# Graph layer on one core: the beginning reordered (zeros without DMA, W1 ahead of W2, rows turned ahead of the first sums, rstd ahead of the additions)

## The reference

```python
agg = jax.ops.segment_sum(edge_attr, dst, num_segments=12500)     # 12500 x 48
h = jnp.maximum(layernorm(x), 0.0)
c = jnp.concatenate([h, agg], axis=1)                             # 12500 x 176
a = silu(c @ W1 + b1)                                             # 256 wide
a = silu(a @ W2 + b2)                                             # 256 wide
out = x + h + a @ W3 + b3                                         # 128 wide
```

## Time and profile before

| | us |
|---|---|
| median of 3 runs | 303.75 (303.45 to 303.93) |
| the profiled execution | 302.05 |
| its span, first to last instruction | 300.3 |
| busy: PE, DVE, ACT, POOL | 283.9, 249.2, 222.5, 112.2 |

### The profile page before, as it was taken

How to read it: one execution, slowest core, us unless ns; L and a number is a source line. 1 busy time by engine, 2 the same in 40 slices (tenths; PEclk the granted TensorE clock), 3 DMA queues, 4 the chain that set the end, 5 groups by cost and what they waited for, 6 DMA issues and landing times.

```text
span 300.3 us, 12188 instructions
## 1 busy us (share of the span) xinstructions
PE 283.9 (95%) x4370; PEld 256.4 (85%) x4371; DVE 249.2 (83%) x615; ACT 222.5 (74%) x434; POOL 112.2 (37%) x243
## 2 busy tenths in 40 slices
PE   7596879999999999999999999999999999999995
PEld 3584758899999999999999999999999999999794
DVE  7956988799888898889988898889988889875551
ACT  5555267887788877888777887888777887789662
POOL 4062345243433435334343334434444343542200
PEclk9899599999999999999999999999999999999999
DMA  6998999368655786557855678556875568631112
GB/s 171 293 264 242 170 215 253 85 204 244 192 164 156 228 244 177 161 158 237 243 162 151 182 240 233 157 155 189 244 232 151 150 203 244 199 109 34 33 32 58
DMA packets 79418, 54.49 MB, mean 181 GB/s; under 512 B 2997, under 2 KB 78863, under 8 KB 79253
## 3 DMA queue, kind: packets, MB, share of 16 engines
q1 hardware_dynamic: 79397, 54.25, 64.9%
HBM read 46.29 MB, written 6.40 MB: 175 GB/s over the span
## 4 chain that ended last, share of the span: by engine, by line
PE 78%; issue 8%; ACT 4%; POOL 3%; DMA 2%; DVE 1%; POOLq 1%; SPq 1%; ACTq 0%; DVEq 0%
PE agg_ps L1054 18%; PE z L1122 16%; PE z L1104 7%; PE z L1105 7%; PE z L1108 7%; PE agg_ps L1057 4%; PE z L1084 4%; PE z L1089 3%; PE z L1085 3%; PE z L1086 3%; PE z L1090 3%; POOL agg_carry L462 3%; PE tp L1068 3%; DMA raw<-in_edge_attr_dram 2%; ACT xn L543 1%
## 5 line engine op out<-in xcount | busy, mean ns | idle before, releaser
L462 POOL TENSOR_TENSOR agg_carry<-staged,agg_carry 48x42 f32 x196 | 69.5, 354 | 91.4 <-ACT staged L511 58.3
L1054 PEld LDWEIGHTS agg_ps<-onehot,raw 128*48 128x48 f32 x1560 | 75.2, 128 | 12.6 <-issue 12.5
L1054 PE MATMUL agg_ps<-onehot,raw 128*48 128x42 f32 x1560 | 78.9, 218 | 3.9 <-DVE onehot L729 3.7
L1057 PE MATMUL agg_ps<-onehot,raw 128*48 128x42 f32 x1568 | 79.3, 218 | 0.6 <-DMA raw<-in_edge_attr_dram 0.6
L729 DVE TENSOR_TENSOR onehot<-window,rel 128x1176 f32<-128x1176 f32 (+1 forms) x57 | 76.9, 1350 | 3.0 <-DVE stats L704 2.7
L1057 PEld LDWEIGHTS agg_ps<-onehot,raw 128*48 128x48 f32 x1568 | 75.8, 129 | 0.8 <-issue 0.8
L443 POOL TENSOR_TENSOR rstd<-vareps,minus_half 112x4 f32<-112x4 f32 (+1 forms) x28 | 39.5, 1411 | 77.4 <-DVE vareps L714 77.4
L1122 PE MATMUL z<-w,h 128*112 128x128 f32 (+1 forms) x448 | 55.9, 278 | 0.8 <-ACT h L575 0.8
L1122 PEld LDWEIGHTS z<-w,h 128*112 128x112 f32 (+1 forms) x448 | 50.4, 176 | 2.4 <-ACT z L571 1.1
L575 ACT ACTIVATE h<-z,b2c 128x448 f32<-128x448 f32 (+1 forms) x56 | 35.4, 633 | 20.3 <-PE z L1108 17.7
L543 ACT ACTIVATE xn<-x_t,nmr,rstd 112x128 f32<-112x128 f32 (+1 forms) x112 | 45.6, 478 | 0.9 <-DVE nmr L722 0.8
(11 more groups left out here) (128 smaller groups left out, 421.6 us busy)
## 6 DMA issues: line engine op xcount, KB each, us to landing
raw<-in_edge_attr_dram SPq DMA_DIRECT2D x55, 672.0 KB, 6.0
x_t<-in_x_dram SPq DMA_DIRECT2D x27, 224.0 KB, 6.3
out_dram<-out_t SPq DMA_DIRECT2D x27, 224.0 KB, 6.1
agg_carry<-agg_carry SPq DMA_DIRECT2D x3, 504.0 KB, 12.8
dst_rows<-in_dst_dram SPq DMA_DIRECT2D x1, 512.0 KB
raw<-in_edge_attr_dram SPq DMA_DIRECT2D x1, 288.0 KB, 3.5
dst_rows<-in_dst_dram SPq DMA_DIRECT2D x1, 256.0 KB, 2.8
out_t<-in_L_gnn_W_dram SPq DMA_DIRECT2D x1, 256.0 KB, 7.4
```

Source lines behind the costliest of these rows:

```text
L462: pool.tensor_tensor(into, staged[:, parity, n, :], into, ALU.add).then_inc(s_added, 1)
L1054: mm = pe.matmul(banks[0:ED, bass.ds(offsets[at - first], WINDOW)], edges, into, start=False, stop=True, skip_group_check=True, tile_posit ...
L1057: mm = pe.matmul(stage[ROW2:ROW2 + ED, at * WINDOW:(at + 1) * WINDOW], edges, into, start=(at == 0 and j == 0), stop=True, skip_group_chec ...
```

## The change

All of it lies in the first steps.

- GpSimd zeroes columns 896 to 8064 of `agg_carry` in four memsets of 1792 columns, behind its iota; ScalarE zeroes all behind, 4544 columns, in one instruction. The three DMAs and the second piece of ScalarE are gone.
- On SP's queue W1 goes ahead of W2, and so do the second half of the edges of batch 1 and `x` of tile 1; W1 and W2 get semaphores of their own. ScalarE and DVE split W1 first and W2 later, `layer1(0)` waits for W1 alone, `layer2(0)` for W2, `activate1(0)` and `layer3(0)` for the small constants.
- ScalarE turns the relative targets of all lots ahead of the staged sums of batch 0 and splits W1 ahead of them too.
- PE turns all four lots of rows ahead of the sums of batch 0, with five matmuls without use between (`WARM1`); eight in place of six ahead of the sums of batch 1 (`WARM2`).
- GpSimd reads the places of batches 0 and 1 at once, then makes `rstd(0)`, then adds batch 0 and batch 1, then makes `rstd(1)`.
- DVE takes the statistics of tile 1 ahead of `carry_over(0)`.
- In DVE's step 1 both one-hots of batch 2 and the split of W2 come ahead of `shift_of_norm(1)`.
- `carry_over` waits for the zeros once, at tile 0.

```diff
-    WARM0, WARM1 = 3, 6
+    WARM0, WARM1, WARM2 = 3, 5, 8
...
-        COPIED, COPIES = 6 * TILE, 3
-        ZEROED = 4 * TILE
+        ZEROED = 18 * TILE
+        CARRY0 = 2 + (ZEROED - POOL_ZEROS) // (4 * TILE)
...
-            sp.dma_start(w2_in, W2.rearrange("(m p) n -> p m n", p=P)).then_inc(s_weights, 16)
-            sp.dma_start(w1x_in, W1[0:D, :]).then_inc(s_weights, 16)
+            sp.dma_start(w1x_in, W1[0:D, :]).then_inc(s_w1, 16)
             for a in (0, ROW2):
-                sp.dma_start(w1e_in[a:a + ED, :], W1[D:D + ED, :]).then_inc(s_weights, 16)
+                sp.dma_start(w1e_in[a:a + ED, :], W1[D:D + ED, :]).then_inc(s_w1, 16)
             load_edges(1, 1, 1)
+            load_x(1, 1)
+            sp.dma_start(w2_in, W2.rearrange("(m p) n -> p m n", p=P)).then_inc(s_w2, 16)
...
-            for c in range(COPIES):
-                sp.dma_start(zeros_to[:, c, :], agg_carry[:, ZEROED + COPIES * COPIED:NT * TILE]).then_inc(s_carry0_dma, 16)
...
             pool.iota(tile_i[:, :], pattern=[[1, TILE]], base=0, channel_multiplier=0).then_inc(s_pool_zero, 1)
+            for a in range(POOL_ZEROS, ZEROED, 4 * TILE):
+                pool.memset(agg_carry[:, a:a + 4 * TILE], 0.0).then_inc(s_carry0, 1)
...
             pool.wait_ge(s_off0, 1)
-            nodes = nodes_of(0)
-            pool.wait_ge(s_carry0, 2)
-            add_staged(0, 0, nodes, range(0, EARLY))
+            nodes = [nodes_of(b) for b in range(2)]
             rstd_of(0, 0)
-            add_staged(0, 0, nodes, range(EARLY, HALF))
+            pool.wait_ge(s_carry0, CARRY0)
+            pool.wait_ge(s_carry0_act, 1)
+            add_staged(0, 0, nodes[0])
+            add_staged(1, 1, nodes[1])
             rstd_of(1, 1)
...
-            clear_carry(ZEROED + COPIES * COPIED, NODES)
+            clear_carry(ZEROED, NODES)
             rel_of(0)
             act.wait_ge(s_dst, 64)
             for c in range(1, ROWS):
                 rows_of(c)
-            clear_carry(POOL_ZEROS, ZEROED)
-            rel_of(1)
-            stage_sums(0, 0)
-            for c in range(2, ROWS):
+            for c in range(1, ROWS):
                 rel_of(c)
-            act.wait_ge(s_weights, WEIGHTS)
...
+            stage_sums(0, 0)
...
             normalize(0, 0)
+            act.wait_ge(s_w2, W2_LOADS)
+            act.activation(w2_hi[:, :, :].rearrange("p m n -> p (m n)"), w2_in.rearrange("p m n -> p (m n)"),
+                           ACT.Copy).then_inc(s_w_hi, 1)
             stage_sums(1, 1)
...
             make_onehot(1, 1, 1)
+            weights1_lo()
             dve.wait_ge(s_smallT, 1)
...
-            weights_lo()
+            load_stats(1, 1)
             dve.wait_ge(s_rel, ROWS)
...
-                    load_stats(1, 1)
                     dve.wait_ge(s_stats, 2)
                     aggregate_stats(1, 1)
                     make_onehot(2, 0, 0)
+                    make_onehot(2, 0, 1)
+                    weights2_lo()
                     shift_of_norm(1, 1)
-                    make_onehot(2, 0, 1)
...
+            turn_rows(1)
             pe.wait_ge(s_off0, 1)
+            turn_rows(2)
+            for _ in range(WARM1):
+                pe.matmul(tp[:, 0:P], ident[:, :], ident[:, :], start=True, stop=True)
             offsets = offsets_of(0)
-            turn_rows(1)
+            turn_rows(3)
             sum_tile(0, 0, offsets)
-            for c in range(2, ROWS):
-                turn_rows(c)
...
-            for _ in range(WARM1):
+            for _ in range(WARM2):
                 pe.matmul(tp[:, 0:P], ident[:, :], ident[:, :], start=True, stop=True)
             sum_tile(1, 1, offsets)
```

More of the change, by code:

```diff
@@ L144, in gnn_kernel @@
         POOL_ZEROS = 2 * TILE
-        COPIED, COPIES = 6 * TILE, 3
-        ZEROED = 4 * TILE
-        assert ZEROED + (COPIES + 1) * COPIED == NT * TILE and LOOP[0] * TILE == ZEROED
+        ZEROED = 18 * TILE
+        CARRY0 = 2 + (ZEROED - POOL_ZEROS) // (4 * TILE)
+        assert (ZEROED - POOL_ZEROS) % (4 * TILE) == 0
         gen_onehot = onehot[:, 2:4].rearrange("p s e w -> p (s e w)")[:, 0:PER * TILE].rearrange(
@@ L204, in rows_turned @@
             return banks[c][:, 0:PER * (P if c < FULL_ROWS else LAST_G)].rearrange("p (j r) -> p j r", j=PER)
-        s_weights = sem("weights_loaded")
+        s_w1 = sem("w1_loaded")
+        s_w2 = sem("w2_loaded")
         s_const = sem("const_loaded")
@@ L451, in nodes_of, with add_staged @@
                 return nodes
-            def add_staged(b, parity, nodes, which=range(HALF)):
+            def add_staged(b, parity, nodes):
                 pool.wait_ge(s_staged, b + 1)
                 wait(pool, s_carried, b)
-                if isinstance(b, int) and b == LATE_ZEROS:
-                    pool.wait_ge(s_carry0_dma, 16 * COPIES)
-                for n in which:
+                for n in range(HALF):
                     wait(pool, s_added, added(b, n))
@@ L465, in step @@
                 parity = turn % 2
-                if has(i, 0, NT):
+                if has(i, 0, NT) and not (isinstance(i, int) and i == 1):
                     nodes = nodes_of(i)
@@ L579, in activate1 @@
                 n = PER * nodes_p(t)
+                if isinstance(t, int) and t == 0:
+                    act.wait_ge(s_const, CONSTS)
                 for m in range(M):
@@ L736, in make_onehot, with weights1_lo, weights2_lo @@
                 onehot_of(i, parity, half).then_inc(s_onehot, 1)
-            def weights_lo():
-                dve.wait_ge(s_w_hi, 4)
[L741 to L747, removed]
+            def weights1_lo():
+                dve.wait_ge(s_w_hi, 3)
+                dve.wait_ge(s_pool_zero, 3)
+                for lo, whole, hi in ((w1x_lo[:, :], w1x_in, w1x_hi[:, :]),
+                                      (w1e_lo[0:ED, :], w1e_in[0:ED, :], w1e_hi[0:ED, :])):
+                    dve.tensor_tensor(lo, whole, hi.bitcast(F32), ALU.subtract).then_inc(s_w_lo, 1)
+            def weights2_lo():
+                dve.wait_ge(s_w_hi, 4)
+                dve.tensor_tensor(w2_lo[:, :, :].rearrange("p m n -> p (m n)"), w2_in.rearrange("p m n -> p (m n)"),
+                                  w2_hi[:, :, :].rearrange("p m n -> p (m n)").bitcast(F32),
+                                  ALU.subtract).then_inc(s_w_lo, 1)
             dve.wait_ge(s_rel, 1)
@@ L857, in carry_over @@
                 dve.wait_ge(s_added, added(t + 1))
-                dve.wait_ge(s_carry0_act, 2)
-                if isinstance(t, int) and t == LATE_ZEROS - 1:
-                    dve.wait_ge(s_carry0_dma, 16 * COPIES)
+                if isinstance(t, int) and t == 0:
+                    dve.wait_ge(s_carry0, CARRY0)
+                    dve.wait_ge(s_carry0_act, 1)
                 wait(dve, s_carried, t)
@@ L1076, in layer1 @@
                 if isinstance(t, int) and t == 0:
[L1077 to L1080, removed]
+                    pe.wait_ge(s_w_lo, 2)
+                    pe.wait_ge(s_w_hi, 3)
                 for m in range(M):
@@ L1095, in layer2 @@
                 n = PER * nodes_p(t)
+                if isinstance(t, int) and t == 0:
+                    pe.wait_ge(s_w_lo, 3)
+                    pe.wait_ge(s_w_hi, 4)
                 pe.wait_ge(s_h1, M * t + M)
@@ L1116, in layer3 @@
                 last = isinstance(t, int) and t == NT - 1
+                if isinstance(t, int) and t == 0:
+                    pe.wait_ge(s_const, CONSTS)
                 pe.wait_ge(s_seeded, t + (2 if last else 1))
```

15 lines of the change are left out of this document (4 added, 11 removed).

## The result

| | before | after |
|---|---|---|
| median of 16 runs each, us | 303.4 (301.89 to 305.94) | 306.33 (305.78 to 307.2) |
| the profiled execution | 302.05 | 305.78 |
| its span | 300.3 | 304.1 |

The ratio is 1.0096 (95% interval 1.0077 to 1.0115): the change makes the kernel slower, by 2.9 us against a forecast of 5.2. The time measured, 306.33, lies in the forecast range (301.0 to 310.3), nearer to rival 2 (307.6) than to the forecast itself (308.9).

The account below looks back on a forecast made before the run. PE is busy throughout from 60 to 280 us, so only the start of layer 1 of tile 1 counts: sums of batch 1 +5.4, with the tail +5.2, on the median 303.75 give 308.9 us; range 301.0 to 310.3.

Parts of the forecast that it names:

- rival 2: DVE's first small steps: DVE gets in at each end of a memset, 4.8 us late, so 307.6 us; chance 0.17.
- the entry: Start of layer 1 of tile 1 on PE, 41.81 us before; its shift was forecast at +5.2 and carried unchanged.
- Rival 1: Beginning of the kernel: the memsets do not hold DVE and the change is faster, 301.6 us; chance 0.28.
- Two of its signs: Trace signs: L643 about 6.5 us, prediction wrong as a whole if it ends before 5; `staged_row` at 15.7.
- one lock: DVE's first small steps: four memsets without pause hold DVE until 10.2 us, making the offsets 6.1 us late.
- 2.3 and 0.7 for the clock: PE from offsets to sums of batch 0: turning and warming 2.3 us, plus 0.7 for the lower clock.
- the bound for full clock: Sums of batch 0 on PE: 2.8 us if the clock is full, against the 3.8 us taken in the forecast.
- Small products: PE between the sums of batches 0 and 1: small products 1.64 us, then 16 warming instructions 2.13 us.
- The tail: End of sums of batch 1 to layer 1 of tile 1, 18.2 us: -1.37 - 0.87 + 0.6 + 1.4 = -0.2.
- The wait of `nmr(1)`: DVE in norm 1: `rstd(1)` behind all fourteen additions makes DVE wait 2.3 us against 0.91, a term of +1.4.
- The shift: Change of the start of layer 1 of tile 1, +5.2 us, carried unchanged to the end and put on 303.75.
- The zero copies: Three DMA transfers removed: the room they leave gives nothing, as no wait up to layer 1 of tile 1 ends with a load.

Follow-up runs that it names:

- before_memsets: The kernel before with only the zeroing changed: four GpSimd memsets behind the iota, ScalarE all behind, no zero copies; 306.36 us, ratio 1.0106.
- late_memsets: The changed kernel with its four memsets moved behind GpSimd's reading of the first places; 301.43 us, ratio 0.9962 to the kernel before.
- one_memset: The changed kernel with its four memsets made into one of 7168 columns; 306.93 us, ratio 1.0148 to the kernel before.
- before_late: The kernel before without zero copies, zeros written by ScalarE and thirteen GpSimd memsets of 48x448 behind the register loads of batch 0; 301.75 us, ratio 0.9936.
- dve_order: `late_memsets` with DVE's second one-hot of batch 3 behind `carry_over(1)` and the first of batch 4 behind the split of `hT` of tile 1; 300.27 us, ratio 0.9894.
- best1: Changed order, `dve_order`'s one-hot move, six unused matmuls behind tile 1's transposes, thirteen late memsets of 448 columns, three more tiles zeroed by ScalarE; 297.21 us, 0.9805 to before.
- warm_entry: `late_memsets` with ten matmuls without use on PE behind the transposes of tile 1; 300.23 us, ratio 0.9914 to the kernel before.

## Why the prediction was right, and where not

**The direction and its cause were right.** The memsets hold DVE, the offsets come late, and PE's chain up to the entry moves with them. `before_memsets` alone shows it, and `late_memsets` is its counterpart. The range says little for it, as it was wide enough to hold a gain too. Rival 1's case, with no hold on the path, is the one that `late_memsets` comes near to: a gain of 1.1 us, where the rival had 1.9 to 2.4.

**Two of its signs failed.** L643 was to last about 6.5 us, and the prediction was to be wrong as a whole if it ended before 5. Its successor L639 lasts 1.82 and ends at 3.66, so by the letter of that sign the prediction fails. In the kernel before the step ahead of it (L641) was the one held up to 3.65; here that step got through in 0.17, so DVE was one step further on when the long memsets began. They held others, from `g_pair` at 4.17 on, so the sign was tied to one instruction where it should have been tied to the chain. `staged_row` came at 14.37, not 15.7. The rest came about: sums 0 at 18.38 (18.5), sums 1 at 25.3 (26), no stop of GpSimd put down to "issue", 1.58 us ahead of `nmr(1)` (2), the entry at 45.24 (47), the clock at 0.50 from 11 to 17.

**The step that failed first was how a held DVE gets in.** The forecast took "one lock" over the whole run of memsets, 6.1 us; its own rival 2 had DVE get in at each end, 4.8 us, and 4.98 was measured. `one_memset` shows what 6.1 belongs to: `staged_row` at 15.32, 5.9 late. The row that spoke for it, L641's 2.02 us, was read as held over several instructions, and such a hold shows again in the kernel after (L639, 1.82 us over the ends of four short memsets). What failed was to carry it over to the four long ones: DVE got in at each of their ends. The Trainium skill, "SBUF — State Buffer", Who interferes with whom, has the ports held "for the whole instruction"; with that the trace agrees four times over for the long memsets, and L639 does not fit it. One detail differed from rival 2: not every small step was held. L645, which has two inputs and 0.16 us, ran while the second memset did, and the third hold fell on the two CASTs, so rival 2's 4.8 was met in part by other steps than it named.

**From the offsets to sums 1.** From the offsets (14.57, the end of `staged_row`) to sums 0 (18.38) PE turned, warmed and turned for 3.8 us, where 2.3 and 0.7 for the clock stood: the clock was at 0.50 from 11 to 17. In return it was back at 1.00 from 18, and sums 0 took 2.7 us, near the 2.8 of the bound for full clock, and not 3.8. Small products 1.64 and warming 2.05 came as forecast, with a gap of 0.57 ahead of them that the sum had left out. Together sums 1 began at 25.3, 1.0 sooner than forecast. Part of that closeness is luck: offsets and sums 0 came 2.2 us cheaper than in the sum, the turning and the gap 1.4 dearer.

**The tail** went from 18.2 to 17.2, by -1.0 and not -0.2. Three of four terms came as they stood: the 1.37 wait of `carry_over(1)` gone, the statistics gone (-0.87), the split of W2 (+0.6). The wait of `nmr(1)` was 1.58, where before had 0.91: +0.67, not +1.4, as GpSimd had six additions of batch 1 done or begun, not four, when it was shut out (for 3.21 us, by two one-hots and the split).

**The shift was not carried unchanged.** At the entry it was 3.43, at tile 2 4.75, later 3.66. The 4.14 us of idle time that the change leaves before the entry, 2.20 before, were followed by the lower clock, and layer 1 of tile 1 ran at it. The prediction looked for the clock only from 12 to 20 us. Of the 2.6 us between 308.9 and 306.33, 1.8 had gone by the entry (5.2 against 3.43), 0.5 lies between the entry and the medians (3.43 against 2.93), and 0.35 is the baseline: the sum put the shift on 303.75, and 16 runs have 303.4.

**The zero copies were valued at nothing, and that was wrong.** No wait ends with one of these loads, and still they cost: the 4.45 us stop is there only with them, and not with DVE's instructions alone. `before_late`, without them and in the old order, is 1.9 us faster than before.

## What to carry to other kernels

A long filler on GpSimd held small DVE instructions (TENSOR_SCALAR, CAST) for as long as its one instruction ran: cut it into short pieces, or put it where DVE's queue has no chain of small steps; the same zeros cost 5.4 us more in one piece than in sixteen. A transfer for which nobody waits can go with stops of engines, so an idle time put down to "issue" is looked at beside what the DMA engines carry at that time before an engine is blamed. And a gain ahead of a gap on PE is counted only behind it: look whether the clock falls there, and close the gap before moving anything else (here `dve_order` gave 0.7% over `late_memsets`, and `best1`, with everything together, stands 2% under before).

## What was not expected of the hardware

- Two DVE instructions were held together behind one memset and both ended with it (4.17 and 4.25 in the kernel after, 5.98 and 5.91 us long in `one_memset`; the second, with two SBUF inputs, may only have queued behind the first); one with two SBUF inputs at 5.73 ran in 0.16 us while a memset ran.
- DVE shuts GpSimd out for longer than one of its own instructions (3.21 us for one addition over two one-hots and a split), while GpSimd's memsets of 448, 1792 and 7168 columns from 4.03 on let DVE in at their ends, and its five from 1.80 on did not (L639, 1.82 us).
- PE idle ahead of the entry was followed by a clock near 0.5 in `before_late` (2.31 us), `dve_order` (2.91), after (4.14) and the profiled execution of `warm_entry` (1.96), but not in `best1` (1.56) nor in before (2.20). The length of the gap alone doesn't order these.
